# A decoder layer on one core: the second attention's transposes, masks and query projections in another order

## The reference, cut to what matters

```python
x = _layernorm(x + _L0_attn_ref(x, w_qkv, w_out, b_out))
x = _layernorm(x + _L0_xattn_ref(x, ctx, ctx, mask, Wq, bq, Wk, bk, Wv, bv, Wo, bo))
x = _layernorm(x + _L0_ffn_ref(x, up, gate, down, router, w_up_s, w_gate_s, w_down_s))

def _L0_xattn_ref(query, key, value, mask, Wq, bq, Wk, bk, Wv, bv, Wo, bo):
    # 16 heads of 16 columns
    q = _split_heads(query @ Wq.T + bq)
    k = _split_heads(key @ Wk.T + bk)
    v = _split_heads(value @ Wv.T + bv)
    scores = jnp.einsum('bhqd,bhkd->bhqk', q, k) * scale
    scores = jnp.where(mask == 0, NEG_INF, scores)
    probs = jax.nn.softmax(scores, axis=-1)
    out = jnp.einsum('bhqk,bhkd->bhqd', probs, v)
    return out.transpose(0, 2, 1, 3).reshape(query.shape[0], -1, D_MODEL) @ Wo.T + bo
```

## Time and profile before

| what | value |
|---|---|
| median of three runs | 427.1 us (426.8 to 427.51) |
| the profiled execution | 428.63 us; span of its trace 426.9 us |
| PE busy | 402.9 us, 94% of the span |
| PEld (weight loads) | 284.7 us, 67% |
| DVE busy | 252.5 us, 59% |
| ACT busy | 192.5 us, 45% |
| POOL busy | 51.2 us, 12% |
| granted TensorE clock, mean | 0.992 |
| scores of the first and of the last slot | 160.76 us and 314.96 us |

### The profile page before, as it was taken

How to read it: one execution, slowest core, us unless ns; L and a number is a source line. 1 busy time by engine, 2 the same in 40 slices (tenths; PEclk the granted TensorE clock), 3 DMA queues, 4 the chain that set the end, 5 groups by cost and what they waited for, 6 DMA issues and landing times.

```text
span 426.9 us, 12682 instructions
## 1 busy us (share of the span) xinstructions
PE 402.9 (94%) x4986; PEld 284.7 (67%) x4987; DVE 252.5 (59%) x729; ACT 192.5 (45%) x575; POOL 51.2 (12%) x79
## 2 busy tenths in 40 slices
PE   8989999999999788999999999999899999999992
PEld 7857878878787565666666666666565475566661
DVE  1357775856667555666668676768673642244443
ACT  1054462443616526677667656667683101111220
POOL 4010001101011001000001010100100054222333
PEclk9999999999999999999999999999999999999998
DMA  7998100000000013050404040920000013121210
GB/s 250 381 390 239 33 3 3 2 5 2 4 3 2 4 38 134 16 185 3 185 2 185 9 178 2 374 110 2 0 4 2 2 61 100 62 62 58 71 44 25
DMA packets 15255, 34.48 MB, mean 81 GB/s; under 512 B 2381, under 2 KB 9150, under 8 KB 13920
## 3 DMA queue, kind: packets, MB, share of 16 engines
q1 hardware_dynamic: 13952, 30.72, 20.5%
q0 software_dynamic: 1104, 2.76, 1.8%
q10 hardware_dynamic: 144, 0.23, 0.2%
HBM read 27.27 MB, written 6.70 MB: 80 GB/s over the span
## 4 chain that ended last, share of the span: by engine, by line
PE 47%; issue 38%; DVE 9%; ACT 4%; POOL 2%; POOLq 0%; DVEq 0%; ACTq 0%
PE banks L444 9%; PE banks L830 5%; PE banks L923 4%; PE banks L899 4%; PE banks L905 4%; PE banks L466 4%; PE banks L521 3%; PE banks L486 3%; ACT p L984 3%; PE banks L842 3%; PE banks L508 3%; DVE p L1155 2%; DVE pT L1164 1%; DVE nm L1147 1%; POOL xb L377 1%
## 5 line engine op out<-in xcount | busy, mean ns | idle before, releaser
L1285 DVE CUSTOM_DVE_ANT_0 p<-banks,mask 112x375 f32<-112x375 f32 x128 | 62.6, 542 | 28.2 <-PE banks L633 28.1
L1038 ACT ACTIVATE p<-p,nm 112x375 f32<-112x375 f32 x128 | 73.8, 603 | 5.3 <-DVE nm L1285 5.2
L1045 ACT ACTIVATE pT<-banks 128x336 f32<-128x336 f32 x96 | 42.3, 442 | 42.2 <-PE banks L653 41.9
L653 PEld LDWEIGHTS banks<-ident,p 112*128 112x128 f32 (+1 forms) x384 | 38.4, 140 | 28.9 <-issue 22.0
L984 ACT ACTIVATE p<-banks,nm 128x112 f32<-128x112 f32 x128 | 43.2, 363 | 31.5 <-DVE nm L1147 31.5
L653 PE MATMUL banks<-ident,p 112*128 112x112 f32 (+1 forms) x384 | 53.2, 266 | 1.9 <-DVE nm L1285 1.5
L444 PE MATMUL banks<-x2T,arena 128*128 128x224 f32 x256 | 52.5, 361 | 0.0
L444 PEld LDWEIGHTS banks<-x2T,arena 128*128 128x128 f32 x256 | 48.9, 194 | 1.8 <-ACT arena L974 0.2
L359 POOL TENSOR_TENSOR rstd<-veps,minus_half 128x1 f32<-128x1 f32 x14 | 7.7, 551 | 286.1 <-DVE veps L1179 286.1
L1140 DVE TENSOR_SCALAR arena<-banks 128x448 f32<-128x448 f32 x32 | 19.8, 620 | 28.9 <-PE banks L444 28.9
L466 PE MATMUL banks<-arena,x2T 128*32 128x256 f32 (+1 forms) x512 | 29.9, 381 | 1.7 <-issue 1.4
(11 more groups left out here) (144 smaller groups left out, 566.8 us busy)
## 6 DMA issues: line engine op xcount, KB each, us to landing
arena<-in_ug SPq DMA_DIRECT2D x8, 1024.0 KB, 5.7
arena<-in_dn SPq DMA_DIRECT2D x8, 512.0 KB, 6.7
mid<-in_ctxT SPq DMA_DIRECT2D x8, 375.0 KB, 3.3
slots_s<-blank SPq DMA_DIRECT2D x14, 128.5 KB
arena<-in_wqk SPq DMA_DIRECT2D x7, 256.0 KB, 6.1
slots_x<-blank SPq DMA_DIRECT2D x14, 128.0 KB
p<-slots_s SPq DMA_DIRECT2D x9, 128.5 KB, 2.0
kT<-slots_x SPq DMA_DIRECT2D x9, 128.0 KB, 2.1
```

The source lines that it names most:

```text
L653: mm = pe.transpose(PE_T2[r][0:k1 - k0, t * S:(t + 1) * S], p2_rows[:, i % RING, k0:k1], ident[0:S, 0:S])
L1038: act.activation(p2[i % RING], p2[i % RING], ACT.Exp, bias=nm2[:, i % H:i % H + 1], scale=-1.0).then_inc(exp2, 1)
L1045: act.activation(pT2[:, i % RING], PE_T2[r][:, 0:KT * S].rearrange("p (k n) -> p k n", k=KT), ACT.Copy).then_inc(pt2_act, 1)
L1285: v.tensor_tensor_reduce(p2[i % RING], PE_S2[r][0:S, 0:S2], bias[:], 1.0, 3e38, ALU.add, ALU.min, accum_out=nm2[:, i % H:i % H + 1]).then_ ...
```

## The change

On TensorE a slot becomes: scores of `n`; places 0, 1 and 2; heads 2 and 3 of slot `n - 1` turned; heads 0 and 1 of slot `n` turned; values of slot `n - 2`. Heads 0 and 1 are therefore turned in the slot of their scores, and wait for its exponentials. VectorE masks head 2 first, then 0, 1 and 3, and ScalarE takes the exponentials in that order; a filler at place 1 needs only head 2 to be masked (it waited for three heads). The query projections move from place 2 of the second slot to place 0 of the third (batches 2 and 4), their evacuation on VectorE from the end of the second slot to place 2 of the third, and `turn_o` of these batches to place 2. On ScalarE the copies of heads 0 and 1 of the slot before come ahead of all exponentials, the key evacuations and `evac_on` come between the exponentials of heads 0 and 1, and the evacuations of the first batch's rows are placed anew. VectorE's copy of head 3 goes behind the value evacuation. The order of the last slots, and where their transposes and values stand among the first pieces of the shared expert, changes with it.

```diff
@@ -236,6 +236,7 @@
         U1_ALL = banks[:, 4 * 512:8 * 512].rearrange("p (c n) -> p c n", c=STRIPS)
         PE_S2, PE_V2, PE_M2 = bank[0:STRIPS], bank[5], bank[6]
         PE_T2 = (bank[4], bank[7], PE_S2[0], PE_S2[1])
+        MASK_ORDER = (2, 0, 1, 3)
         PE_L2 = PE_S2[2]
 
         def block1(j, full=True):
@@ -635,7 +636,7 @@
                 mm.then_inc(scores2, 1)
 
             def turn2_(n, r):
-                pe.wait_ge(exp2, n * STRIPS + r + 1)
+                pe.wait_ge(exp2, n * STRIPS + (3 if r < 2 else 4))
                 if n == 0 and r == 0:
                     pe.wait_ge(ot1[0], B)
                     pe.wait_ge(ot1[1], B)
@@ -646,7 +647,7 @@
                 elif r == 1:
                     pe.wait_ge(pt2_act, n * 3 - 1)
                 elif n + 1 < SLOTS:
-                    pe.wait_ge(max2, (n + 1) * STRIPS + r - 1)
+                    pe.wait_ge(max2, (n + 1) * STRIPS + 3)
                 i = n * STRIPS + r
                 for t in range(KT):
                     k0, k1 = KEYS[t][0], min(KEYS[t][0] + 128, SP)
@@ -720,7 +721,7 @@
 
                 b, g = n // GROUPS, n % GROUPS
                 if place == 1:
-                    pe.wait_ge(max2, n * STRIPS + 3)
+                    pe.wait_ge(max2, n * STRIPS + 1)
                 if b == 0:
                     between_first(g, place)
                 if (g, place) == (0, 1) and b >= 1:
@@ -738,10 +739,10 @@
                     project_k(1, b + 1)
                 if (g, place) == (1, 1) and b >= 3:
                     turn_x2(b - 3)
-                if (g, place) == (1, 2) and b in (2, 4):
+                if (g, place) == (2, 0) and b in (2, 4):
                     pe.wait_ge(k_sb, (b + 2) * KC)
                     project_q(b // 2 + 1)
-                if (g, place) == (2, 0) and b >= 1:
+                if (g, place) == (2, 2 if b in (2, 4) else 0) and b >= 1:
                     if b in (2, 4):
                         pe.wait_ge(q_sb, b // 2 + 2)
                     elif b + 1 < B:
@@ -775,23 +776,18 @@
 
             for n in range(SLOTS):
                 score2(n)
-                if n >= 1:
-                    turn2_(n - 1, 0)
-                    turn2_(n - 1, 1)
-                between(n, 0)
+                for place in range(3):
+                    between(n, place)
+                if n == SLOTS - 1:
+                    out2(NT - 2)
                 if n >= 1:
                     turn2_(n - 1, 2)
                     turn2_(n - 1, 3)
-                between(n, 1)
-                between(n, 2)
+                turn2_(n, 0)
+                turn2_(n, 1)
                 if n >= 2:
                     value2(n - 2)
-            out2(NT - 2)
-            turn2_(SLOTS - 1, 0)
-            turn2_(SLOTS - 1, 1)
             value2(SLOTS - 2)
-            turn2_(SLOTS - 1, 2)
-            turn2_(SLOTS - 1, 3)
 
             def logits_first():
 
@@ -846,14 +842,16 @@
             pe.wait_ge(w_loaded["shared"], 32)
             pe.wait_ge(max2, SLOTS * STRIPS)
             shared(0, 0, range(0, 1))
+            turn2_(SLOTS - 1, 2)
+            turn2_(SLOTS - 1, 3)
+            shared(0, 0, range(1, 2))
             value2(SLOTS - 1)
-            shared(0, 0, range(1, 2))
             turn_x2(NT - 2, bank[1])
+            shared(0, 1, range(0, 1))
             pe.wait_ge(y2, NT - 1)
             turn_o(B - 1)
-            shared(0, 1, range(0, 1))
+            shared(0, 1, range(1, 2))
             turn_on(B - 1)
-            shared(0, 1, range(1, 2))
             logits_first()
             out2(NT - 1)
             shared(1, 0)
@@ -1034,7 +1032,7 @@
 
             def exps2(n, r):
                 i = n * STRIPS + r
-                act.wait_ge(max2, i + 1)
+                act.wait_ge(max2, n * STRIPS + MASK_ORDER.index(r) + 1)
                 act.activation(p2[i % RING], p2[i % RING], ACT.Exp, bias=nm2[:, i % H:i % H + 1], scale=-1.0).then_inc(exp2, 1)
 
             def evac_pt(n, r):
@@ -1045,42 +1043,38 @@
                 act.activation(pT2[:, i % RING], PE_T2[r][:, 0:KT * S].rearrange("p (k n) -> p k n", k=KT),
                                ACT.Copy).then_inc(pt2_act, 1)
 
-            def before_exps(n):
-
-                b, g = n // GROUPS, n % GROUPS
-                if b == 0 and g >= 2:
-                    evac_x1(g + 2)
-                if g == 1 and 1 <= b < B - 1:
-                    evac_k(0, b + 1)
-
             def between(n, place):
 
                 b, g = n // GROUPS, n % GROUPS
                 if (g, place) == (0, 1) and b == 0:
                     evac_x1(2)
-                if (g, place) == (1, 0) and b == 0:
+                if (g, place) == (1, -1) and b == 0:
                     evac_x1(3)
-                if (g, place) == (1, 0) and 1 <= b < B - 1:
-                    evac_k(1, b + 1)
-                if (g, place) == (3, 0) and b == 0:
+                if (g, place) == (1, 2) and b == 0:
+                    evac_x1(4)
+                if (g, place) == (2, 2) and b == 0:
+                    evac_x1(5)
+                if (g, place) == (3, -1) and b == 0:
                     evac_x1(6)
+                if (g, place) in ((0, 0), (1, 0)) and 1 <= b < B - 1:
+                    evac_k(g, b + 1)
                 if (g, place) == (3, 0) and b >= 1:
                     evac_on(b - 1)
 
             for n in range(SLOTS):
-                before_exps(n)
                 if n >= 1:
                     evac_pt(n - 1, 0)
+                    evac_pt(n - 1, 1)
+                between(n, -1)
+                exps2(n, 2)
                 exps2(n, 0)
-                if n >= 1:
-                    evac_pt(n - 1, 1)
+                between(n, 0)
                 exps2(n, 1)
-                between(n, 0)
                 if n >= 1:
                     evac_pt(n - 1, 2)
-                exps2(n, 2)
                 between(n, 1)
                 exps2(n, 3)
+                between(n, 2)
             evac_pt(SLOTS - 1, 0)
             evac_pt(SLOTS - 1, 1)
             evac_pt(SLOTS - 1, 2)
@@ -1339,10 +1333,8 @@
                     evac_x2(b - 3)
                 if (g, place) == (1, 0) and b >= 3:
                     ln2_b(b - 3)
-                if (g, place) == (1, 4) and b in (2, 4):
+                if (g, place) == (2, 2) and b in (0, 2, 4):
                     evac_q(b // 2 + 1)
-                if (g, place) == (2, 2) and b == 0:
-                    evac_q(1)
                 if (g, place) == (2, 0) and b >= 1:
                     evac_ot(b - 1)
                 if (g, place) == (2, 4) and b >= 1:
@@ -1354,15 +1346,15 @@
 
             for n in range(SLOTS):
                 between(n, 0)
+                mask_and_max(n, 2)
                 mask_and_max(n, 0)
+                between(n, 1)
                 mask_and_max(n, 1)
-                between(n, 1)
-                mask_and_max(n, 2)
                 between(n, 2)
                 mask_and_max(n, 3)
+                between(n, 3)
                 if n >= 1:
                     evac_pt2(n - 1)
-                between(n, 3)
                 between(n, 4)
             ln2_add(NT - 2)
             ln2_a(NT - 2)
```

## The result

The changed kernel takes 445.11 us (median of four runs, 442.76 to 445.91) against 426.95 before: ratio 1.041, 95% interval 1.038 to 1.045. It is slower by 18.2 us. Its profiled execution took 442.76 us, span 440.8, mean granted clock 0.991; it is the fastest of the four.

What follows compares the result with a forecast made beforehand. A full TensorE bounds the second attention; new waits cost at once. Batches 0 to 7 and the last slot, 1.5 + 1.9 + 1.7 + 3 x 1.6 + 0.8 + 1.5 + 1.1, add 13.3 us to 427.1: 440.4 us, range 433 to 446.

Steps and rivals of the forecast that it cites:

- Chain inside a slot: From the scores' start: first mask 1.14 us, first exponential 1.73, three exponentials over 3.33, new pair from 3.42.
- The sign that was named: Plain third slots: some 4.7 us, with TensorE idle ahead of heads 0 and 1 until ScalarE's exponential releases it.
- First, second and plain third slots: Second attention: 5.18 us; 5.18, or 5.44 with a normalisation from batch 3 on; and 4.73.
- Fourth slot: Output projection waits for ScalarE's evacuation until 3.24 us; slot 6.12 us, or 5.07 in batch 1 without that projection.
- Query third slots: Third slots of batches 2 and 4, with the query projections and their later evacuation on VectorE: 6.32 us.
- Batches: Batches 1 to 4: 20.2, 22.8, 21.5 and 23.1 us; batch 0 taken as +1.5.
- Batch 7: First three slots of batch 7: 4.73 + 5.1 + 4.73 = 14.6 us against 13.12, +1.5.
- Last slot: TensorE empty from 1.21 to 3.24 us, waiting for the evacuation; last normalisation, routing and experts come 1.1 us later.
- the upper bound of 446: Whole kernel: normalisation later in five slots (4.0 us) and every pair at 0.64 (1.2 us) give 445.6; range 433 to 446.
- TensorE stays full: Rival for the second attention: exponentials keep up, 18.6 us a batch against 19.91, time 417 us; chance 0.06.
- Copies come late: Rival: ScalarE's and VectorE's copies of the old pair delay the next scores; 31 slots add 15 us, 456 us; chance 0.04.
- The clock falls: Rival: clock at 1.2 GHz through the second attention's batches, some 125 us in all, 566 us; chance 0.02.

Runs made afterwards that it cites:

- the second experiment: Changed kernel with ScalarE's evacuation of the turned output moved ahead of all exponentials of the fourth slot: 440.16 us, ratio 1.031.
- the sixth: Changed kernel with heads 0 and 1 turned in the next slot again and the turned output's evacuation ahead of the exponentials: 429.08 us, ratio 1.002.
- eighth experiments: Kernel before with query projections moved to the third slot, and head 2 first in third and fourth slots of batches 0 to 6: 424.71 us, ratio 0.992.
- the seventh experiment: Changed kernel with masks and exponentials in the order of heads 0, 1, 2, 3 again, waits to match: 454.93 us, ratio 1.065.
- the fifth experiment: Changed kernel with one more, unread key projection in place 0 of each of batch 7's first three slots: 447.97 us, ratio 1.048.
- the first experiment: Changed kernel with heads 0 and 1 turned again in the slot after their scores, right behind the next scores: 435.02 us, ratio 1.019.
- the fourth: Kernel before with only the query projections of batches 2 and 4, their evacuation and the output's turn moved within the third slot: 425.44 us, ratio 0.996.

## Why the prediction was right, and what it missed

Slower was right, and for the reason given: with heads 0 and 1 turned in their own slot TensorE waits for that slot's masks and exponentials. Undoing just that takes back 10.1 of 18.2 us, and undoing the late evacuation as well leaves no difference that can be told. The predicted 13.3 us were 4.9 too few. By its steps:

- **Chain inside a slot**: right. Masks, exponentials and waits stand where slot 0 put them; the first exponential came at 1.75 for 1.73, the new pair at 3.87 for 3.87 in the first slot and at 3.41 for 3.42 in the third. The sign that was named, a rest ahead of heads 0 and 1, is plain only in second slots; in third ones the rest stands ahead of the value projection, and the exponentials hold the pair by a few hundredths.
- **First, second and plain third slots**, 5.18, 5.18 or 5.44, and 4.73: measured 5.31, 5.30 or 5.43, and 4.85. The mis-sized term is the new pair: 0.60 was read from pairs that start without waiting, but behind its wait it takes 0.72 to the values (277.31 to 278.03 in the second slot, 282.16 to 282.88 in the third). In the fourth slot, where neither pair waits, both take 287.71 to 288.95 = 1.24, for 1.21. That is 0.12 in first slots, plain third ones and the second ones of batches 1 and 2, some 1.5 us in batches 1 to 6.
- **Fourth slot**, 6.12 and 5.07 in batch 1: 6.07 and 5.08, with the evacuation of line 1004 as the releaser. Right.
- **Query third slots**, 6.32: 6.43. The second slots without them, "like any other": 5.30 in batch 2, but 5.78 in batch 4, 0.35 over the other batches.
- **Batches**: 20.5, 23.1, 21.7 and 23.6 for batches 1 to 4 against 20.2, 22.8, 21.5 and 23.1; batch 0 gained 1.9 for 1.5.
- **Batch 7**: 16.45 for 14.6. This is the largest miss. Taken at the second experiment's 5.19 and 4.85, its second and third slots are 1.56 shorter, so most of it is the fall of the clock in slot 29 and at the start of slot 30.
- **Last slot**: a rest of 2.12 us for 2.0, and 1.08 us more behind it for 1.1. Right.

Together the stretch gained 16.06 for 12.2, and the tail 1.08 for 1.1. The remaining 1.0 us of the median's rise is not placed; the other three runs of the median have mean granted clocks of 0.983 to 0.986, where the runs of before have 0.989 to 0.995, so falls of the clock such as those below are the likely place, which no trace of those runs shows. Two more runs of the changed kernel fit: 443.52 us at 0.991 and 445.76 at 0.983. That 445.1 still lies below the upper bound of 446 is in part luck: the bound was made of a later normalisation and slower pairs, not of a fall of the clock.

The rivals. *TensorE stays full* did not happen in the change, and the sixth and eighth experiments show what it would have needed: with both pairs taken from the slot before, plain third slots have 4.15 to 4.21 us and no rest on PE. The Trainium skill's rule on rotating banks (Perfetto Trace Analysis, Matmuls) did not bring it about; the rows show waits for masks and exponentials in its place. *Copies come late* did not happen: scores start right behind the values, 0.72 after them (282.88 to 283.60). *The clock falls* was priced as all or nothing, 125 us at 0.02. The step that failed is its sentence that new rests are under 0.8 us except in the last slot: slots 28 to 30 rest 0.87, then 1.22 and 0.59, then 1.33, and slot 1 rests 1.01 (0.76 before). Its own chain gives 1.0 in slot 28, from the end of the scores (0.83) to head 2's bank (1.83). The fall came in one place, not throughout: slot 29 at a mean granted clock of 0.80 and slot 30 at 0.92, between the 1.2 and the 2.4 GHz level, worth about 1.5 us.

## What to carry to other kernels

When work is moved to an earlier slot, count the whole chain that it now waits for, from the slot's first instruction, and lay it beside the fillers that are to cover it; here 3.4 us of chain met 0.4 to 2.3 us of fillers. A change of many parts can hold a good one: moving the query projections, and masking head 2 first in the two slots whose fillers need its bank, made the kernel 3.2 us faster without the rest. If a group will start behind a wait, its duration should be read from rows in which it does.

## What the runs showed of the hardware

The granted clock falls to its half level in single places, and not in every execution of the same instructions. In the changed kernel it is 0.50, the 1.2 GHz level, from 321.20 to 322.50 us, in slot 29. The most frequent fall is outside the change. Before the sixteen products of the first attention's output projection TensorE rests for 3.03 us and works for 1.0; the sixteen took 5.41 us before and 3.72 after; the rows on PE, of before and then of after:

```profile
147.10 5.41 PE L521 MATMUL banks<-arena 128*128 128x256 f32 x16
```

```profile
145.22 3.72 PE L522 MATMUL banks<-arena 128*128 128x256 f32 x16
```

That is 1.69 of the 3.24 us by which the profiled execution of the change was ahead at the first scores. Eight of the ten profiled executions show this fall, with 5.01 to 5.79 us for the sixteen; only the changed kernel's and the seventh experiment's don't. So it may be part of why the changed kernel's profiled execution stands 2.35 below its median, which no trace of its other runs shows.

Other falls came in slots 1 and 2, in slots 29 and 30 and after the last slot's rest, each in some kernels' profiles and absent in others with the same code there. Where a kernel with the same code kept its clock, the cost can be read: 1.56 us in slots 29 and 30 of the changed kernel, 1.34 in slot 2 of the fifth experiment. No length of the rests ahead of them tells them apart here. Slot 2 fell behind rests of 0.52 and 1.01 in the fifth experiment, while the changed kernel had the same rests and kept 1.00; it fell behind 0.70, 0.45 and 0.65 in the first. Slot 29 fell behind 1.22 and 0.59 in the changed kernel, and kept 1.00 behind 2.21 in the seventh experiment. The kernel before and those of the fourth and eighth experiments show no fall from the first scores to the last; nor does the second experiment's, which rests as the changed kernel does. The Trainium skill (TensorE: Matmul & The Clock Gate, A second HAM failure mode: psum-queue depth-cycling) describes another kernel, in bf16, in which short idle times between groups of matmuls made the clock swing between its two levels. The short rests ahead of these falls agree with that (0.80 in slot 29); it doesn't say why the second experiment's kernel, with the same rests, kept 1.00, and that stays open.

The Trainium skill (TensorE: Matmul & The Clock Gate, PE-mode transpose) says that transposes don't count as activity in the same way. Four heads turned in a row ran at the full clock in nearly every slot of the changed kernel (1.00 in batches 1 to 6), and slot 29 fell to 0.82 in the first experiment too, where only two heads are turned in a row; so no cost of four in a row shows here.
